# Storing a layer's features with nodes on partitions, and adding them after the turn instead of before it

## The reference, cut to what matters

```python
h = jnp.maximum(_layernorm(x), 0.0)                  # the normalised features
g = relu(_gcn(h, W1, b1, src, dst, norm))            # layer 1
g = relu(_gcn(g, W2, b2, src, dst, norm))            # layer 2
x = x + (h + g) * 0.5
h = jnp.maximum(_layernorm(x), 0.0)
agg = segment_sum(edge_attr, dst)                    # 64 attributes of an edge
y = leaky_relu(concat([h, agg, u]) @ w1 + c1)
y = leaky_relu(y @ w2 + c2)
x = x + y @ w3 + c3
```

## Time and profile before

| | us |
|---|---|
| median of 3 runs | 1178.48 |
| profiled execution | 1181.4 |
| its span, first to last instruction | 1179.6 |
| setup | 0 to 257 |
| layer 1 and its end | 262 to 751 |
| layer 2 and the rest | 751 to 1179.6 |

### The profile page before, as it was taken

One profiled execution on the slowest core, in us unless ns is written; L12 is line 12 of the kernel. 1 busy time (PEld: TensorE's weight loads), 2 busy tenths in 40 slices (PEclk: granted clock), 3 DMA queues, 4 the chain that ended last, 5 costly groups with the idle time before them and its releaser, 6 DMA issues. The chain is left out here.

```text
span 1179.6 us, 30059 instructions
## 1 busy us (share of the span) xinstructions
PE 1075.1 (91%) x9799; PEld 707.8 (60%) x9800; DVE 721.8 (61%) x1203; ACT 534.0 (45%) x1243; POOL 255.6 (22%) x184
## 2 busy tenths in 40 slices
PE   1999899866999999999999997599999999999995
PEld 1999889865666666666666654454444444444442
DVE  5558565539999999999999926422332323332232
ACT  1012345507888888888888844312121211212212
POOL 3445201535962322222332000000000000000000
PEclk9999899985999999999999998899999999999997
DMA  6999799700566666666555569977887777777710
GB/s 219 304 372 320 247 302 303 237 17 17 192 207 199 198 198 198 198 198 198 190 188 186 184 196 285 311 221 253 263 247 236 225 229 227 237 224 243 240 36 20
DMA packets 225240, 252.62 MB, mean 214 GB/s; under 512 B 13898, under 2 KB 192063, under 8 KB 225048
## 3 DMA queue, kind: packets, MB, share of 16 engines
q1 hardware_dynamic: 110372, 144.56, 38.4%
q10 hardware_dynamic: 109828, 96.49, 25.3%
q0 software_dynamic: 4976, 10.71, 2.8%
HBM read 161.74 MB, written 90.00 MB: 213 GB/s over the span
## 5 line engine op out<-in xcount | busy, mean ns | idle before, releaser
L974 ACT CAST adj_all<-win_p 128x392 f32 x784 | 342.6, 497 | 52.1 <-PE win_p L1023 33.8
L1023 PEld LDWEIGHTS win_p<-adj_all,st 128*128 128x128 f16 x3136 | 215.4, 101 | 145.2 <-ACT adj_all L974 29.5
L1023 PE MATMUL win_p<-adj_all,st 128*128 128x98 f16 x3136 | 256.8, 213 | 23.0 <-ACT adj_all L974 16.3
L924 DVE TENSOR_TENSOR st<-iota_lo,code 128x2048 f16 x196 | 243.2, 1241 | 15.6 <-ACT code L963 8.1
L1038 PE MATMUL dense_p<-adj_all,g_hi 128*128 128x448 f16 x686 | 241.0, 351 | 1.2 <-DVE total L935 0.9
L1038 PE MATMUL dense_p<-adj_all,g_lo 128*128 128x448 f16 x686 | 241.6, 352 | 0.0
L1632 PE MATMUL dense_p_b<-adj_all,g_hi 128*128 128x512 f16 (+1 forms) x637 | 231.9, 372 | 3.7 <-issue 3.4
L1632 PE MATMUL dense_p_b<-adj_all,g_lo 128*128 128x512 f16 (+1 forms) x637 | 231.7, 371 | 0.0
L754 PE MATMUL agg_p<-ahot,arows 128*64 128x64 f32 x3240 | 203.3, 226 | 13.6 <-DVE ahot L465 7.6
L754 PEld LDWEIGHTS agg_p<-ahot,arows 128*64 128x64 f32 x3240 | 198.2, 141 | 19.0 <-issue 17.9
L924 DVE TENSOR_TENSOR adj_all<-iota_mv,code 128x1568 f16 x196 | 193.2, 986 | 0.0
(11 more groups left out here) (204 smaller groups left out, 810.4 us busy)
## 6 DMA issues: line engine op xcount, KB each, us to landing
adj_d<-adj_all ACTq DMA_DIRECT2D x14, 5488.0 KB, 19.5
adj_all<-adj_d SPq DMA_DIRECT2D x11, 6272.0 KB, 23.5
arows<-in_edge_attr_dram SPq DMA_DIRECT2D x45, 960.0 KB
adj_all<-adj_d ACTq DMA_DIRECT2D x1, 6272.0 KB, 35.2
disb<-dis_d SPq DMA_DIRECT2D x24, 256.0 KB, 5.7
arows<-in_edge_attr_dram SPq DMA_DIRECT2D x9, 640.0 KB
h<-in_x_dram ACTq DMA_DIRECT2D x4, 768.0 KB
hT_d<-hT ACTq DMA_DIRECT2D x12, 256.0 KB, 6.2
```

The source lines that it names most:

```text
L924: ins = nc.vector.tensor_tensor(hot[:, bass.ds((b * BG + j) % 2, 1), u, :, :] .rearrange("p a w (n t) -> p (a w) n t", t=2), iota[:, :].re ...
L974: nc.scalar.copy(adj[:, bass.ds(b % 2, 1), :, bass.ds(j * GN + k * WN, WN)] .rearrange("p b h d -> p (b h) d"), win_p[:, k % 4, 0:WP * MV] ...
L1023: ins = nc.tensor.matmul(win_p[:, k % 4, 0:WP * MV] .rearrange("p (h c t) -> p h c t", c=WP, t=PN)[:, :, c, :], st[:, odd, k // UW, pair, ...
```

## The change

`h` is stored as it lies, nodes on partitions, straight behind ScalarE's normalisation; PE's transposes, ScalarE's copies, and the buffer and semaphores for them are taken out. In layer 2 `h0` is loaded with nodes on partitions, and VectorE adds half of it to `xt` ahead of its wait for the transposes, in place of the addition to `hn`; PE's `turn_to_nodes` waits for ScalarE's `hn` itself.

```diff
-        hT_d = scratch("hT_d", (F, NP), F32)
+        h_d = scratch("h_d", (NP, F), F32)
...
-            hT = sb("hT", [P, 2, TB * P], F32, ph)
...
                 def keep(i):
                     k, n = BATCH[i]
-                    act.wait_ge(s_turned, i + 1)
-                    if i >= 2:
-                        act.wait_ge(s_hT[i % 2], 16 * (i // 2))
-                    nc.scalar.copy(hT[:, i % 2, 0:n * P], tp[:, i % 2, 0:n * P]).then_inc(s_kept, 1)
-                    act.wait_ge(s_kept, i + 1)
-                    act.dma_start(hT_d[:, k * P:(k + n) * P], hT[:, i % 2, 0:n * P]).then_inc(s_hT[i % 2], 16)
+                    act.wait_ge(s_h, i + 1)
+                    act.dma_start(h_d[k * P:(k + n) * P, :].rearrange("(c p) f -> p c f", p=P), h[:, k:k + n, :]
+                                  ).then_inc(s_kept, 16)
...
-                for q in range(2):
-                    act.wait_ge(s_hT[q], 16 * len(BATCH[q::2]))
+                act.wait_ge(s_kept, 16 * len(BATCH))
...
-                def turn_nodes(i):
-                    k, n = BATCH[i]
-                    pe.wait_ge(s_h, i + 1)
-                    if i >= 2:
-                        pe.wait_ge(s_kept, i - 1)
-                    for c in range(n):
-                        ins = nc.tensor.transpose(tp[:, i % 2, c * P:(c + 1) * P], h[:, k + c, :], ident[:, :])
-                    ins.then_inc(s_turned, 1)
...
-                    if 15 <= m < 15 + len(BATCH):
-                        turn_nodes(m - 15)
...
-                            sp.dma_start(h0[:, h, 0:w], hT_d[:, cols]).then_inc(small_ready[h], 16)
+                            sp.dma_start(h0[:, h, 0:w].rearrange("p (c f) -> p c f", f=F),
+                                         h_d[cols, :].rearrange("(c p) f -> p c f", p=P)).then_inc(small_ready[h], 16)
...
-                            dve.wait_ge(hn_ready, c + 1)
-                            nc.vector.tensor_tensor(hn[:, 0:w], hn[:, 0:w], h0[:, h, 0:w], ALU.add
-                                                    ).then_inc(comb_ready, 1)
+                            link(nc.vector.scalar_tensor_tensor(
+                                out=xt[:, h, 0:n, :], in0=h0[:, h, 0:w].rearrange("p (c f) -> p c f", f=F), scalar=0.5,
+                                in1=xt[:, h, 0:n, :], op0=ALU.mult, op1=ALU.add))
                             dve.wait_ge(tpa_done, c + 1)
...
-                            pe.wait_ge(comb_ready, c + 1)
+                            pe.wait_ge(hn_ready, c + 1)
```

More of the change, by code:

```diff
@@ L284, in build @@
             s_h = sem("s_h1", ph)
-            s_turned = sem("s_turned1", ph)
             s_kept = sem("s_kept1", ph)
-            s_hT = [sem(f"s_hT{k}", ph) for k in range(2)]
             s_edges = sem("s_edges", ph)
@@ L1289, in second_layer_and_mlp @@
                 hn_ready = sem("hn_ready", ph)
-                comb_ready = sem("comb_ready", ph)
                 tpa_done = sem("tpa_done", ph)
```

## The result

The changed kernel has a median of 1173.73 us over 5 runs (1170.36 to 1174.73) against 1178.48 for the kernel before (5 runs, 1177.75 to 1178.62): ratio 0.9939, 95% interval 0.9921 to 0.9957, so 0.6% faster. The forecast was 1170.0 us within 1165 to 1177, a gain of 8.5 us. The medians here are 4.75 us apart, a ratio of 0.9960; the recorded ratio stands for 7.2 us (5.1 to 9.3), and the record doesn't show why it is larger than that of the medians. Two further series gave the same pair 0.9919 (0.9906 to 0.9931) and 0.9916 (0.9903 to 0.9929), that is 9.6 and 9.9 us. So the size was about right by the ratios, and nearly twice too large by the first medians alone. The steps that made it were not all mine: one term is 2 us too large, and 3 us came from a place I had taken for idle.

A forecast was written before the change was run, and what follows sets the result against it. PE was taken as the bound (91% busy; late in the setup VectorE waits for it). Terms 6.7 + 1.1 + 0.7 = 8.5 us; 1181.4 - 8.5 = 1172.9 profiled answers to a median of 1170.0, range 1165.0 to 1177.0.

The forecast's parts named there:

- unit 28 at 191 to 192 and L639 near 250: Setup signs: PE's 60-matmul unit 28 starts at 191 to 192 us; VectorE's line L639 comes near 250.
- Transposes ahead of `cnt` free: Setup: PE's next step waits for VectorE's `cnt` anyway, so removing the transposes before it gains 0.
- Setup, TensorE, 6.7 us: Setup: without its transposes PE starts unit 28 at 191.6 instead of 198.29, a gain of 6.7 us.
- Unit 28 to the end alike: Setup: from unit 28 on both orders run alike, 8 units, a gap, the last turn and VectorE's last write.
- ScalarE and GpSimd not late: Setup: ScalarE's scaling starts at about 184.5 instead of 199.16; GpSimd's chain ends 14 us sooner, needing only some 5.
- GpSimd beside VectorE costed at 0: Setup: GpSimd's `g_lo` slows VectorE's hots, but its lead of some 2.9 us covers it; cost 0, at worst 3.5 us.
- Rival 3, PE starves: Setup, 158 to 198 us: PE lacks instructions; one stall gives 1176.6, a second 1183.2; chances 0.10 and 0.05.
- GpSimd's chain ended at 254.30 + 0.87: Setup of the kernel before: GpSimd's chain ended there, ahead of VectorE's last write at 256.61 + 0.17.
- Rival 4: Setup: something unseen ends it, so only 1.8 us comes, giving 1176.7; chance 0.05.
- Transfers 0: Setup store in 512-byte rows: 3 us more DMA time, hidden by loads running six units ahead; cost 0, perhaps 2 us.
- Layer 2, 1.1 us: Layer 2, under the multiply: moving VectorE's addition off the path to the transposes gains 0.1 us in each of 11 chunks.
- Tail, 0.7 us: Tail behind the last multiply: the uncovered addition leaves and the new one hides behind `linear`, a gain of 0.7 us.

The follow-up runs named there:

- three transposes back: Changed kernel with the first three groups of transposes put back behind units 15, 16 and 17, results unused: 1172.58 us, ratio 0.9913 to the kernel before.
- setup only: Changed setup and store, with the load and addition in layer 2 of the kernel before: 1175.33 us, ratio 0.9927 to the kernel before.
- scaling held back: Changed kernel with one more wait on `s_bound` ahead of ScalarE's scaling of the features: 1180.19 us, ratio 0.9964 to the kernel before.
- layer 2 only: Kernel before with its old setup and the changed load and addition in layer 2: 1182.13 us, ratio 0.9983 to the kernel before.
- 2-KB rows: Changed kernel with `h_d` laid out so that batches are stored and loaded in 2 KB rows: 1165.57 us, ratio 0.9921 to the kernel before.
- `cnt` first: Kernel before with VectorE's `cnt` at m=15 and the edge codes at 16 and 17: 1181.88 us, ratio 1.0069 to the kernel before.
- small steps one unit later: Changed kernel with PE's small setup steps from m=18 and VectorE's from m=19 one unit later: 1166.25 us, ratio 0.9935 to the kernel before.

## Why the prediction was right, and where it wasn't

Taken from the first pair of profiles, 10.5 us apart. Until VectorE's `shift`, which lies ahead of the first transpose that left, the two executions are already 1.7 us apart:

```profile
141.84 0.21 DVE L554 SCALAR_TENSOR_TENSOR shift_x<-mean_var,rstd_x 128x49 f32<-128x49 f32 x1
```

```profile
140.13 0.21 DVE L551 SCALAR_TENSOR_TENSOR shift_x<-mean_var,rstd_x 128x49 f32<-128x49 f32 x1
```

That is chance, like the 2.9 and 2.8 us by which the profiled runs miss their medians: the two repeats of the changed kernel have `shift` at 141.09 and 141.22. So two signs of the forecast, unit 28 at 191 to 192 and L639 near 250, were met by 192.3 and 250.31 with 1.7 us of luck.

- **Transposes ahead of `cnt` free:** right. L784 came at 155.46 behind `cnt`, with TensorE idle in front of it; putting them back changed nothing.
- **Setup, TensorE, 6.7 us:** too large. Counted from `shift`, unit 21 gained 0.15 us (26.08 for 26.23) where I had 2.7; unit 28 came 56.45 us behind `shift` before and 192.3 - 140.13 = 52.2 after: 4.3 us, and VectorE's last instruction 114.77 and 110.18: 4.6. The step that failed is this one, "units 19 and 20 from 157.55 on end at 164.55": I gave them 3.50 us each, and they took 9.35 for both, behind 3.69 us of idle time that I had myself put in front of L802. In the stretch of that gap the clock was granted at 0.82, a mean between the levels of 1.2 and 2.4 GHz, where the kernel with three transposes back had 1.00. It was not the only limit, though: with the clock whole, waits for `next_sb` and `mxT` took its place. VectorE had less slack there than I gave it. In four more profiles with the changed setup, series 1 and 3 (both repeats, setup only, scaling held back), the same stretch from `shift` took 109.6 to 112.95 us, and 114.93 with the setup of before (layer 2 only), so the gain at VectorE is between 1.8 and 5.1.
- **Unit 28 to the end alike:** right. From L803 to VectorE's end 65.25 us, and 66.66 before, of which the two groups of transposes behind it were 1.1.
- **ScalarE and GpSimd not late:** right; scaling at 185.24 against a forecast of 184.5. The last two issues of the store took 4.16 us, and ScalarE still idled 9.62 us in front of `norm`. GpSimd's last instruction came 11.5 us sooner, not 14.
- **GpSimd beside VectorE costed at 0:** right. The hots that ran beside `g_lo` took 2.13, 2.77, 1.97, 1.64 and 2.15 us, 2.13 in the mean, and TensorE ran its ten units through them without a wait. The Trainium skill, "SBUF — State Buffer", section "Who interferes with whom", by which these hots are blocked, agrees in direction, and in size for one of the five at most (2.77; the longer value was 2.56); VectorE's lead of some 2.9 us covered it, so the 5.0 that I had worked out beside it didn't come.
- **Rival 3, PE starves:** didn't come. From 124.60 on no idle time of TensorE in the setup ended with nothing shown. Its sign did come, a clock below full between 150 and 220, but behind the wait for `cnt`.
- **"GpSimd's chain ended at 254.30 + 0.87":** this step failed too, and what it hid was the second part of the gain. The chain ended at 259.9, with the drain, and it was the last of the setup; VectorE's write at 256.61, on which I made the whole term, was not. Rival 4 had said that something I don't see ends the setup, and priced it at a gain of 1.8 only, since it left the unseen thing where it was. But it hung on the edit: ScalarE's copies were in front of it, and it moved by 11.5 us. That was worth 4.29 - 1.27 = 3.0 us on top of VectorE's.
- **Transfers 0:** right, by the 2-KB rows. At first sight the 0.8 us by which the start of layer 2 was longer (from VectorE's first product with `disb` at layer 1's end, L1153, to its `c_sb`, 766.73 - 718.05 = 48.7 before and 757.83 - 708.32 = 49.5 after) could be a cost of the 512-byte rows. The setup-only kernel, with 2-KB reads there, has 49.7, and the kernel before with `cnt` first 49.9. It is scatter.
- **Layer 2, 1.1 us:** right. From VectorE's `c_sb` at layer 2's start to the tail's `lin_p`, three profiles with the old layer 2 have 384.2 us in the mean (383.9 to 384.5), eleven with the new one 383.2 (382.9 to 383.7): 0.9.
- **Tail, 0.7 us:** right where it is made, most of it given back later. `lin_p` to `tpa` is 0.72 shorter in ten of the eleven profiles with the new order; with 2-KB rows it took 2.94, at half the clock from `lin_p` on. But from `lin_p` to the last store it is 24.5 to 24.7 us with the old order and 24.3 to 24.5 in eight of the eleven with the new one (two have 23.3, one 25.4; the means are 24.6 and 24.3). The clock makes the difference. In stretches of 2 us counted from `lin_p`, it is back at 1.00 from 16 us on in the kernel before (0.67 in the stretch ahead), from 14 us on in the first profile after (0.68 ahead), and in the two repeats only between 16 and 18 us (0.95 and 0.99 there, 0.50 ahead). The same eight matmuls took 3.82 us before, 3.70 in the first profile after, and in the repeats 4.79 and 4.65:

```profile
1155.39 3.70 PE L1585 MATMUL zz_p<-a,w_sb 128*128 128x512 f32 x8 [0.22 <-DVE a L1463]
```

```profile
1159.71 4.79 PE L1585 MATMUL zz_p<-a,w_sb 128*128 128x512 f32 x8
```

The products at L1564, at the whole clock (1.98 us for four) in the first profile after and in the first repeat alike, don't make it: there the tail is 23.3 and 24.3 us.

Summed from `shift` on in the first pair: 4.6 at VectorE and 3.0 at the drain make 7.6 for the setup (forecast 6.7, setup-only kernel 8.6), and 0.9 and 0.3 in the mean make 1.2 for layer 2 and the tail (forecast 1.8, layer-2-only kernel 2.0): 8.8, against 8.5 forecast and 7.2, 9.6 and 9.9 by the three ratios. With 1.8 to 5.1 at VectorE it is 6.0 to 9.3. Two errors of opposite sign, of 2.1 and 3.0 us, make that agreement look better than the working was; that they nearly cancel is luck. Why the first comparison gives less than the two later ones stays open; its interval of 5.1 to 9.3 us and theirs, from 8.2 and from 8.4 up, overlap by about 1 us.

## What to carry to other kernels

At a stage that ends with a meeting of all engines, ask of each queue when it can leave, not when its last instruction ended; on GpSimd that was 4.7 us later here, and it was the last. An engine that you free may sit at the head of another engine's chain, so follow the chain to the stage's end before you call it slack, and when your own change opens a gap in front of TensorE, price both the wait and the clock behind it, then ask which wait comes next. Here closing the gap gave back the clock and still nothing that the time shows, since TensorE then waited for VectorE elsewhere.

## What the runs showed of the hardware that I had not expected

- GpSimd's drain at the block's end took 5567 to 5588 ns in all fourteen profiles, with its last work a 0.9-us operation behind DMAs that it had issued by index. It ended 4.7 us behind that operation. The drains of VectorE and ScalarE took 184 to 186 and 419 to 476 ns and ended within 0.1 us of their last instructions (before: 256.79 for 256.78, and 221.92 for 221.84). What GpSimd's waits for isn't shown.
- TensorE, idle for 3.5 to 5.6 us with the DMA queues full, was granted a lower clock around or behind the gap (0.82 to 0.97 over 15 or 21 us), and the two units behind it took 8.3 to 9.4 us in place of 7.2. Gaps of about 1 us (three transposes back) and one of 1.88 us in the kernel before did not do this; 1.85 and 1.97 us in front of `mxT` (the two kernels with the small steps one unit later) were followed by a unit of 5.23 us in place of 3.5. So the length of the one gap doesn't settle it.
- In the tail, reaching a point sooner at the low clock gave most of the time back: in nine of eleven profiles with the new order the clock's return didn't come sooner with the work.
